# Layer 0 of a two-layer graph network: ReLU and the high half of h at the end of ScalarE's step, and one chain of LayerNorm factors for a group of four graphs

## The reference, cut to what matters

```python
h = jnp.maximum(_layernorm(x), 0.0)
m = h @ map_w.T + map_b
n = sem / norm                            # sem: m by heads; norm: its length in each head
cos_adj = (n @ n.T > THRESHOLD)           # masked by adj
q, k = m @ q_w.T + q_b, m @ k_w.T + k_b
p_attn = softmax(where(sm, NEG, q @ k.T / 8)) * keep
adj = cos_adj * p_attn
x = x + relu((adj @ (h @ gcn_map_w.T + b)) @ gcn_W.T / (adj.sum(-1) + 1))
```

## Time and profile before

| | |
|---|---|
| median of three executions | 2969.36 us |
| the profiled execution | 2969.26 us |
| its span (first to last instruction) | 2967.5 us |
| layer 0's group loop with projections | about 120 to 1955 us of the span |
| TensorE busy | 94% of the span |
| VectorE, ScalarE, GpSimd busy | 65%, 58%, 54% |
| mean granted TensorE clock | 0.982 |

### The profile page before, as it was taken

One profiled execution on the slowest core, in us unless ns is written; L12 is line 12 of the kernel. 1 busy time (PEld: TensorE's weight loads), 2 busy tenths in 40 slices (PEclk: granted clock), 3 DMA queues, 4 the chain that ended last, 5 costly groups with the idle time before them and its releaser, 6 DMA issues. The chain is left out here.

```text
span 2967.5 us, 65887 instructions
## 1 busy us (share of the span) xinstructions
PE 2799.9 (94%) x21907; PEld 1593.8 (54%) x21910; DVE 1925.8 (65%) x6356; ACT 1718.2 (58%) x4891; POOL 1587.9 (54%) x4656
## 2 busy tenths in 40 slices
PE   5999999999999999999999999967999999999997
PEld 2455555555555555555555555543555555565654
DVE  4466666666666666666666666655666666666764
ACT  3455655565555556555655565545666666666663
POOL 1566566556655665566556655623555455445541
PEclk8999999999999999999999999978999999999998
DMA  4233343333334333334333334235665656556552
GB/s 126 55 87 87 88 102 87 87 90 100 87 88 90 98 87 91 91 95 87 91 94 92 87 93 97 72 93 118 159 152 151 158 144 155 151 144 160 149 141 64
DMA packets 555745, 318.39 MB, mean 107 GB/s; under 512 B 452496, under 2 KB 454032, under 8 KB 555408
## 3 DMA queue, kind: packets, MB, share of 16 engines
q1 hardware_dynamic: 555408, 314.19, 42.7%
HBM read 146.32 MB, written 67.11 MB: 72 GB/s over the span
## 5 line engine op out<-in xcount | busy, mean ns | idle before, releaser
L501 ACT ACTIVATE probs<-probs,negmax 128x128 f32<-128x128 f32 x1024 | 398.3, 390 | 413.5 <-DVE negmax L119 413.5
L627 DVE SCALAR_TENSOR_TENSOR cpT_lo<-ps_pt,cpT_hi 128x512 f16<-128x512 f32 x256 | 177.1, 692 | 536.7 <-ACT cpT_hi L508 536.7
L161 PE MATMUL ps_pj<-wm_hi,hT 128*128 128x512 f16 x1024 | 326.5, 380 | 16.6 <-DVE wm_lo L670 15.0
L161 PE MATMUL ps_pj<-wv_hi,hT 128*128 128x512 f16 x1024 | 326.8, 380 | 0.0
L161 PE MATMUL ps_pj<-hT,wk_hi 128*128 128x512 f16 x1024 | 305.8, 380 | 0.0
L161 PE MATMUL ps_pj<-hT,wq_hi 128*128 128x512 f16 x1024 | 304.5, 379 | 0.0
L1103 ACT ACTIVATE l_probs<-l_probs,l_negmax 128x128 f32<-128x128 f32 x512 | 199.1, 390 | 150.8 <-DVE l_negmax L119 150.8
L1072 POOL TENSOR_TENSOR l_xres<-l_xres,l_bo_rows 128x512 f32<-128x512 f32 x128 | 172.8, 1350 | 151.2 <-DMA l_xres<-x_scratch 151.2
L508 ACT ACTIVATE cpT_hi<-ps_pt 128x512 f16<-128x512 f32 x256 | 152.0, 594 | 165.1 <-PE ps_pt L837 165.1
L413 POOL TENSOR_TENSOR v_lo<-v,v_hi 128x512 f16<-128x512 f32 x128 | 143.5, 1121 | 194.0 <-ACT v_hi L492 193.9
L119 DVE CUSTOM_DVE_ANT_0 probs<-ps_sc,mask 128x128 f32<-128x128 f32 x1024 | 234.0, 285 | 3.9 <-PE ps_sc L829 3.9
(11 more groups left out here) (196 smaller groups left out, 7272.8 us busy)
## 6 DMA issues: line engine op xcount, KB each, us to landing
xg<-in_x SPq DMA_DIRECT2D x32, 1024.0 KB, 5.6
xres<-in_x SPq DMA_DIRECT2D x128, 256.0 KB, 2.9
x_scratch<-o_sb SPq DMA_DIRECT2D x128, 256.0 KB, 2.1
xg<-x_scratch SPq DMA_DIRECT2D x128, 256.0 KB, 3.0
l_xres<-x_scratch SPq DMA_DIRECT2D x128, 256.0 KB, 3.4
out<-l_o_sb SPq DMA_DIRECT2D x128, 256.0 KB, 3.7
mask_u<-in_adj SPq DMA_DIRECT2D x32, 64.0 KB, 5.2
hT<-h SPq DMA_TRANSPOSE x128, 3.1
```

Of the source, the lines that this page charges most:

```text
L161: last = pe.matmul(out, a(kt), b(kt), start=(n == 0), stop=(n == 3 * kts - 1))
L501: last = nc.scalar.activation(probs[:, i], probs[:, i], ACT.Exp, bias=negmax[:, u % 2, i:i + 1], scale=-1.0, accum_out=zsum[:, u % 4, hh:h ...
L627: nc.vector.scalar_tensor_tensor(cpT_lo[:], ps_pt[:].rearrange("p (h n) -> p h n", h=HB), F16_SCALE, cpT_hi[:], ALU.mult, ALU.subtract).th ...
```

## The change

ScalarE: `relu` and `h_high` of graph hj = (u + 2) % 8 stay in step u, but go from the first half of it to its end, behind `exps(n+1)`, `k_copy` and `n_high`. VectorE: `h_low` of a graph comes one step later (hj = (u + 1) % 8) and stands directly behind `select_similar`, not behind `row_max`. SyncE: `transpose_h` comes one step later too, so graph 0 in step 7, and graphs 1, 2, 3 in steps 0, 1, 2 of the next group (before: steps 6, 7, 0, 1). Statistics are taken two each in steps 4 and 5 (before: 2, 1, 1 in steps 4, 5, 6). GpSimd makes one chain of factors for four graphs in step 6 (before: two chains for two graphs, in steps 5 and 7), and the mask moves from step 6 to step 5. The entry to the loop is adapted.

```diff
@@ SyncE
                 transpose_n(0, j)
-                if j >= 2:
-                    transpose_h(1, j - 2)
+                if j == 2:
+                    transpose_h(1, 0)
@@ SyncE, group(t)
-                    hg, hj = (t + 1 + (u + 2) // 8, (u + 2) % 8)
+                    hg, hj = (t + 1 + (u + 1) // 8, (u + 1) % 8)
                     if hj < QUAD and hg < GROUPS:
                         transpose_h(hg, hj)
@@ GpSimd, group(t)
-                    if ahead and u in (5, 7):
-                        factors(t + 2, u - 5, 2)
-                    if proj and u == 6:
+                    if proj and u == 5:
                         convert_mask(t + 1)
+                    if ahead and u == 6:
+                        factors(t + 2, 0, QUAD)
                     if u % 2:
                         add_residual(t, u // 2)
@@ ScalarE, group(t)
-                    hg, hj = (t + 1 + (u + 2) // 8, (u + 2) % 8)
-                    normed = hj < QUAD and hg < GROUPS
-                    if normed:
-                        relu(hg, hj)
                     if proj and u >= KT:
                         q_copy(t + 1, u - KT)
-                    if normed:
-                        h_high(hg, hj)
                     cpT_high(n)
                     if n + 1 < 8 * GROUPS:
                         exps(n + 1)
...
                     if proj and 2 <= u < 2 + QUAD:
                         n_high(t + 1, u - 2)
+                    hg, hj = (t + 1 + (u + 2) // 8, (u + 2) % 8)
+                    if hj < QUAD and hg < GROUPS:
+                        relu(hg, hj)
+                        h_high(hg, hj)
@@ VectorE
-                if b >= 2:
-                    h_low(1, b - 2)
+                if b == 2:
+                    h_low(1, 0)
@@ VectorE, group(t)
                     select_similar(n)
+                    hg, hj = (t + 1 + (u + 1) // 8, (u + 1) % 8)
+                    if hj < QUAD and hg < GROUPS:
+                        h_low(hg, hj)
                     if proj and 3 <= u < 3 + QUAD:
                         n_low(t + 1, u - 3)
                     cpT_low(n)
                     if n + 1 < 8 * GROUPS:
                         row_max(n + 1)
-                    hg, hj = (t + 1 + (u + 2) // 8, (u + 2) % 8)
-                    if hj < QUAD and hg < GROUPS:
-                        h_low(hg, hj)
...
-                    if ahead and u == 4:
-                        stats(t + 2, 0)
-                    if ahead and 4 <= u < 7:
-                        stats(t + 2, u - 3)
+                    if ahead and u in (4, 5):
+                        stats(t + 2, 2 * (u - 4))
+                        stats(t + 2, 2 * (u - 4) + 1)
```

## The result

The changed kernel takes 3108.43 us (median of four), the kernel before 2969.82 us in the same comparison. The ratio is 1.0463, with a 95% interval of 1.045 to 1.0477: 4.6% slower. The forecast was 3062.8 us with a range of 3008 to 3089: the right direction, and the largest loss in the right place, but 45 us too little, and the time lies outside the range.

The account below looks back on a forecast made before the run. TensorE's own work was taken to bound all but one step a group. From 2969.3 us, minus 78.6 (ReLU's wait), plus 125.6 (stall) and 46.5 (clock), came 3062.8 us, range 3008 to 3089.

Parts of the forecast that it names:

- ReLU's wait goes: In step 6, ScalarE's ReLU no longer holds up TensorE by waiting for GpSimd's factors: gain 78.6 us.
- ScalarE's and VectorE's other moves cost nothing: In the other steps, moved ReLU, halves and statistics fall where the engines wait anyway: cost nothing.
- The transpose behind the store stalls step 3: On SyncE in step 2, graph 3's transpose lands late: TensorE stalls 4.05 us in 31 groups, 125.6 us.
- TensorE's clock: Behind step 3's stall TensorE runs at a lower clock: 1.5 us in each of 31 groups, 46.5 us.
- Step 0 and the x load: On SyncE, graph 1's transpose lands just when project_m starts and the x load is issued about when it was: nothing.
- Rival A: In step 3, the stall comes without the lower clock: 3016.3 us, chance 0.20.
- Rival B: In step 3, graph 3's transpose is not late and the whole gain returns: 2890.7 us, chance 0.06.
- Rival C: In step 6, the chain of factors is still late behind mask and residual: toward 3141 us, chance 0.04.

Follow-up runs that it names:

- e5: The changed kernel with the transpose of h before the store in even steps and the x and mask loads behind graph 3's transpose: 2900.9 us, ratio 0.9755.
- e7: The kernel before with only the change's factors (one chain for four graphs), mask and statistics: 3101.0 us, ratio 1.0432.
- e6: e5 with GpSimd's factors (two chains), mask and VectorE's statistics in the places of the kernel before: 2899.3 us, ratio 0.9754.
- e3: The changed kernel with 16 matmuls of unused result put on TensorE right before project_m of graph 3: 3037.8 us, ratio 1.0229.
- e1: The changed kernel with SyncE issuing the transpose of h before the store and residual load in even steps: 2934.5 us, ratio 0.988.
- e8: The changed kernel with even steps' transpose of h between store and residual load, and add_residual ahead of normalise in step 1: 3000.2 us, ratio 1.0098.
- e2: The changed kernel with the transpose of h ahead of the store in step 2 alone: 2947.8 us, ratio 0.992.

## Why the prediction was right or wrong, point by point

1. *ReLU's wait goes, 78.6 us come back.* Right. The wait is gone, and e5 shows the gain once nothing else stands in the way. That the changed order of mask and residual leaves the chain in time was right as well: no wait of L461 was left. e7 shows how much that rested on the ReLU's new place.

2. *ScalarE's and VectorE's other moves cost nothing.* Right: steps 4 to 7 stand at 7.07 us, and e5 and e6, with all these moves, run at 2901 and 2899 us.

3. *The transpose behind the store stalls step 3.* Right in mechanism, place and count, and close in size: 4.05 us forecast, 4.36 measured (4.24 in e3), 135.1 instead of 125.6 us. The single times were met within 0.1 us in the common case. What was short: h_low's collision cost 0.48 and not 0.37, and in ten groups the landing took over 4 us instead of 3.6 (4.6 us for the one issued at 399.68 us), which lifts the mean above the common case.

4. *TensorE's clock.* **This is the step that failed in size.** 1.5 us a group was forecast with bounds 0 and 2, 2.07 was measured: 64.2 us instead of 46.5. I had taken the price from one stretch of 3.4 us at 0.55 and from one cost of 1.2 us. Those were single drops after single spells; the clock stayed down about twice as long in more than half of the groups, and my upper bound of 2 us left it out. The trace of the kernel before does hold such a case, right behind the stretch of the earlier trace rows, which I passed over. Behind an idle spell of 3.52 us the clock is at half for 6.83 us, with 5.80 us of work in it:

```profile
2937.14:2943.97 6.83, 5.80 (x26) 3.28 (x26) 2.48 (x11) 0.68 (x2) 0.00 (x0) 0.50 0.18 62
```

Rival A, the stall without the clock (3016 us), is refuted: e3 is that case made by hand, and at 3037.8 us it lies where A comes to with the stall, the other steps and the gain as e3 has them (3016.3 + 5.8 + 13.3 + 0.7 = 3036).

5. *Step 0 and the x load.* **This is the step that failed in judgement.** The term was put at nothing. For graph 1's transpose in step 0 the working said "lands just when project_m starts" and I took 0. There was no slack, and a landing varies to one side only: 13 waits of 0.3 to 1.7 us, 13.6 us in all by the distances, and 3.1 us around step 7. This term decides about the range: stall and clock together came to 6.43 us a group, which is still its top (6.4), and the 17.1 us of the other steps, for which it had no room, carry the time beyond it. And "the x load is issued about when it was" was true, but its order against graph 3's transpose had turned round. That cost nothing in the changed kernel, where the store's wait let the load finish first, but it cost 33 us in e1, where it didn't.

The sum of the differences: 9.5 (stall) + 17.7 (clock) + 17.1 (other steps, 216.4 − 199.3) + 0.7 (gain 77.9 instead of 78.6) = 45.0 us. The measured time differs by 138.6 and the forecast by 93.5: 45.1 us. Nothing is left over.

Rival B (faster, 2891 us) was refuted for this kernel and is what e5 comes to when the queue is put right. Rival C (factors still late) was refuted. What stays open: why the clock falls earlier behind some spells, later behind others and not at all behind a few of the same length. I made no run that sets the moment of a spell.

## What to carry to other kernels

When a step is moved, every instruction that it issues moves along the queue of its own engine: read what stands ahead of each in its new place, and what that waits for. Here one DMA issue moved past a wait for GpSimd, and turned a gain of 2.4% into a loss of 4.6%. Where a forecast says "arrives just in time", count the late side of the scatter as a cost, and where a stall of 2 us or more on TensorE is forecast, add a slower clock behind it, and let the upper bound be the longest stretch seen behind one such spell (here 6.8 us, 3.4 us lost; the mean was 2.07 in the changed kernel).

## What the runs showed of the hardware that I had not expected

- The clock can stay at 1.2 GHz for about 6.8 us at the end of and behind an idle spell of 3.8 us, although TensorE worked without a gap for 5.8 of them: stretches of this length came in 18 of 31 groups, and half as long ones in 12. The long ones are those that began 0.79 us or more before TensorE went on (46 of 46 drops in all runs, against none of 61).
- Idle spells between 2.5 and 3.3 us were followed by a drop in 11 of 16 cases (e8), spells of 2.0 to 2.4 us in six of 13 (e1, e2 and e8), and spells up to 1.9 us in none.
- Useless matmuls in a stall that can't be avoided pay: 16 of them a group saved 71 us, 2.3% (e3 against the changed kernel).
- A transposing DMA that lands in 3.0 us alone landed 4.6 to 7.0 us after its issue when it was issued some 1.9 us behind a load of 1 MB (e1, 30 groups). In two of these groups its issue itself took 2.4 and 3.2 us instead of some 1.24.
- A link of GpSimd's chain, 0.20 us by itself, took 0.53 to 0.73 us beside a VectorE instruction that reads two inputs from SBUF (h_low, n_low), in all 124 cases of the changed kernel.
